# A float32 recommendation tower on one core: who subtracts the rest of layer 0's squares, and behind which instruction

## The chip, the cores and the metric

One core of a Trainium2 chip runs the program. The metric is the device time of one execution in microseconds (us), as the median of several runs. The core has a tensor engine (TensorE, PE in the rows; its weight loads are PEld), a vector engine (VectorE, DVE), a scalar engine (ScalarE, ACT), GpSimd (POOL) and SyncE (SP), which issues most of the DMAs. They run side by side, each through a list of its own, and meet only at semaphores.

## The reference

For 2048 samples, 39 embedding rows of 16 numbers are gathered from 39 tables: `e[b, f, d]`. Then follow three layers of a compressed interaction network:

```
x0 = xk = e
for W, b in ((w0, b0), (w1, b1), (w2, b2)):
    z = relu(einsum('bhd,bkd,hks->bsd', x0, xk, W) + b)      # s = 128
    xk, direct = z[:, :64], z[:, 64:]                        # the last layer: direct = z
```

The direct parts are summed over d (256 values per sample), joined with 16 dense numbers, and go through a small perceptron (512, 256, 1). All of it is float32.

## The kernel before

**Tiles and chunks.** A tile is 128 samples (`TB`); of its 16 embedding positions d, four at a time form a chunk of N = 512 columns (4 x 128). There are 16 tiles of 4 chunks, 64 chunks in all. The quarter c = 0 to 3 says which chunk of its tile it is. `Fori` loops run over the tiles in the middle; the first and the last are written out.

**Layers 1 and 2** of a chunk are 20 steps: a step multiplies two rows of x0 (spread over the partitions by DMA, `xb`) with xk on VectorE (`product`, L752, 128 x 1024), and TensorE contracts the product with W. `KIND = "GVPVGPVGVPVGVGVGVGVP"` gives each step's kind. In a P step the float32 product goes to TensorE as it is (L887). In a V or G step it is split: ScalarE rounds it to float32r (`round_`, L558, the high half `Ph`), the remainder (`Pl`, the low half) is subtracted by VectorE in a V step (L757) and by GpSimd in a G step (`low`, L414), and TensorE takes the high half with two weights (L897) and the low half with one (L907). VectorE's order is the step's product first and then the low half of the step before, where that is a V step. So the low half of step 18 comes behind the product of step 19 and ahead of the next chunk's first product. Steps 6 to 9 already belong to layer 1 of the next chunk. At step 8 ScalarE evacuates layer 1's result: `direct1` (L570), which waits for TensorE's steps up to 5, then `upper` (L561) and `lower` (L564), which VectorE needs for step 10. The code has ScalarE do this ahead of the rounding of step 8.

**Layer 0** is computed from squares: (a + b) squared holds the product of a and b. For the chunk two ahead, TensorE transposes the embedding into the bank `aux_ps` at step 0 (L863), ScalarE copies it out (L540, L541), TensorE makes sums of pairs in the same bank (`sums`, L870, at `SUM_AT`), ScalarE squares them (`square`, L545, at `SQUARE_AT`), and TensorE contracts the squares with w0 (`contract0`, L875, L877, at `CONTRACT_AT`). There are 780 pairs, which is six groups of 128 (float32) and a rest of 12. The rest goes in float32r: the sums of the 12 pairs stand three times in the bank, at partitions 0, 32 and 64, `sqx` is the rounded square of 76 partitions (L549), and its rows 0 to 11 are then replaced by the remainder of the rounding: the exact square, minus the rounded one. One matmul (L877), at step 19, takes it all.

**What sets the order around the change.** All of it is written out by hand in step numbers. `rest_squares` (ScalarE, step 18, ahead of the rounding of step 18) squares the bank into `sqx` and, once more, its first 12 rows into SBUF (`rest_sq`, L550). `rest_low` (L420) is GpSimd's subtraction, `sqx[LOWS] = rest_sq - sqx[LOWS]`, at `REST_AT = 17` behind the low half of step 17 and ahead of the gathers of steps 18 and 19 and of the low half of step 0. For the first two chunks, in the prologue, VectorE does it (L764). TensorE's `contract0` of the rest waits for `rest_ready`; the next transposes wait for `rest_square`, since they overwrite the bank. In quarter 1 the next tile's embedding is split too: ScalarE's L531 at step 15 and L534 at step 17, GpSimd's L424 at step 18.

Of the kernel before, what the change touches and what calls it, by code (L numbers as in the profile page):

```python
# [13 lines left out]
GAP = 32  # L14
# [14 lines left out]
LOWS = slice(0, REST)  # L29
ROWS = slice(2 * GAP, 2 * GAP + NF)  # L30
assert 0 < REST <= GAP
# [16 lines left out]
CONTRACT_AT = [6, 8, 10, 12, 14, 16, 19]  # L48
REST_AT = 17
DIRECT0_AT, UPPER0_AT, LOWER0_AT, RELU2_AT, DIRECT1_AT, RELU1_AT = 2, 3, 4, 5, 8, 8  # L50
# [82 lines left out]
def build(nc, ids, tables, x0_dram, sel0_d, inc_d, w0a_d, w0b_d, w1_d, w2_d, b_d, dense_d, wt1_d, wx_d, bt1_d, wt2_d, bt2_d,  # L133
          wt3_d, out):
    ctx = ExitStack()
    with ctx:
# [16 lines left out]
        sel0 = sb("sel0", [128, 2 * N], F32R)  # L153
        rows = sb("rows", [ROWS.stop, N])
        sq = sb("sq", [R0, 2, N])
# [18 lines left out]
        bt2 = sb("bt2", [128, H2 // 128])  # L174

        rows_sb, rest_sq = rows[ROWS, :], rows[LOWS, :]

# [144 lines left out]
        def _(sp):  # L322
# [9 lines left out]
            def write_rows(T, c):  # L332

                sp.wait_ge(rows_ready, T * CPT + c + 1)
                sp.dma_start(x0_dram[c % SCRATCH, 0:NF, :], rows_sb).then_inc(rows_written, 16)
                sp.wait_ge(rows_written, 16 * (T * CPT + c + 1))
                sp.sem_inc(rows_settled, 1)
# [54 lines left out]
        def _(pool):  # L392
# [23 lines left out]

            def rest_low(T, chunk):
                pool.wait_ge(rest_high, T * CPT + chunk + 1)
                pool.wait_ge(rest_square, T * CPT + chunk + 1)
                pool.tensor_tensor(sqx[LOWS, :], rest_sq, sqx[LOWS, :], ALU.subtract).then_inc(rest_ready, 1)  # L420

            def low_emb(T):
# [48 lines left out]
            def tile(T, ref, fields, first=False, last=False):  # L471

                todo = [list(f) for f in fields]
                for c in range(CPT):
                    for k in range(STEPS):
                        if KIND[k] == "G" and (CPT * ref + c, k) in STEPSET:
                            low(T, ref, c, k)
                        if k == REST_AT and not (last and c >= 2):
                            rest_low(T, c + 2)
                        if (c, k) == NEXT_IDS_AT and todo[2]:  # L480
                            next_ids(T + 2)
                        part = min(c, 1) if (c, k) < NEXT_IDS_AT else 2
                        n = GATHERS[c].count(k) + (first and c == 0 and k in FOLD1_AT)
                        for f in todo[part][:n]:
                            gather(f)
                        todo[part] = todo[part][n:]
                        if c == 0 and not first and k in FOLD1_AT:
                            if k == FOLD1_AT[0]:
                                pool.wait_ge(z2_read, T * CPT)
                            fold1(T - 1, FOLD1_AT.index(k) + 1)  # L490
                        if c == 2 and k == FOLD1A_AT:
                            pool.wait_ge(z2_read, T * CPT + 2)
                            fold1(T, 0)
                        if c == 1 and k == FOLD0A_AT:
                            pool.wait_ge(z0_read, T * CPT + 2)
                            pool.wait_ge(z1_read, T * CPT + 2)
                            fold0(T, 0)
                        if c == CPT - 1 and k in FOLD0_AT:
                            if k == FOLD0_AT[0]:
                                pool.wait_ge(z0_read, T * CPT + CPT)  # L500
                                pool.wait_ge(z1_read, T * CPT + CPT)
                            fold0(T, FOLD0_AT.index(k) + 1)
                        if c == 1 and k == LOW_AT and not last:
                            low_emb(T + 1)
# [16 lines left out]
        def _(act):  # L521
# [15 lines left out]
            def copy_x(T, number):  # L537

                act.wait_ge(aux_ready, T * PER["aux"] + number + 1)
                act.activation(rows_sb, aux_ps[0:NF], ACT.Copy).then_inc(rows_ready, 1)  # L540
                act.activation(x2[:, :], aux_ps[0:R2], ACT.Copy).then_inc(aux_read, 1)  # L541
# [5 lines left out]
            def rest_squares(T, chunk, number, bank=aux_ps):  # L547
                act.wait_ge(aux_ready, T * PER["aux"] + number + 1)
                act.activation(sqx[:, :], bank[0:REST0], ACT.Square).then_inc(rest_high, 1)  # L549
                act.activation(rest_sq, bank[LOWS], ACT.Square).then_inc(rest_square, 1)  # L550

# [163 lines left out]
        def _(dve):  # L715
# [44 lines left out]

            def rest_low(chunk):
                dve.wait_ge(rest_high, chunk + 1)
                dve.wait_ge(rest_square, chunk + 1)
                dve.tensor_tensor(sqx[LOWS, :], rest_sq, sqx[LOWS, :], ALU.subtract).then_inc(rest_ready, 1)  # L764

# [11 lines left out]

            rest_low(0)
            dve.wait_ge(xk1_ready, 1)
            waiting = None  # L780
            for s in range(PRE):
                dve.wait_ge(xb_in[s], 32)
                product(0, 0, -1, L1B + s)
                if s == PRE - 1:
                    rest_low(1)
                if waiting:
# [5 lines left out]
            def tile(T, ref, first=False, last=False):  # L792
                for c in range(CPT):
                    end = last and c == CPT - 1
                    waiting = None
                    for k in range(STEPS):
# [15 lines left out]
                        if waiting:  # L812
                            low(*waiting)
                        waiting = (T, ref, c, k) if KIND[k] == "V" else None
                    if waiting:
                        low(*waiting)
# [43 lines left out]
        def _(pe):  # L860
# [100 lines left out]
            def tile(T, ref, first=False, last=False):  # L961
                late = None
                for c in range(CPT):
                    no0 = last and c >= 2
                    for k in range(STEPS):
                        number = AUX * (c + 2)
                        aux = T * PER["reads"] + READS * (c + 2)
                        if k == TRANSPOSE_AT and not no0:
                            pe.wait_ge(emb_full, T + 1 + (c + 2) // CPT)
                            pe.wait_ge(emb_low, T + 1 + (c + 2) // CPT)  # L970
                            pe.wait_ge(aux_read, aux)
                            pe.wait_ge(rest_square, T * CPT + c + 2)
                            transposes((c + 2) % CPT)
# [125 lines left out]
```

## Time and profile before

| | |
|---|---|
| median of 3 runs | 2473.49 us (2471.82 to 2473.76) |
| the profiled execution | 2473.12 us, its span 2471.3 us |
| busy: TensorE, its weight loads | 2417.4 us (98%), 1646.7 us (67%) |
| busy: VectorE | 2224.4 us (90%) |
| busy: ScalarE | 1733.9 us (70%) |
| busy: GpSimd | 1948.2 us (79%) |
| mean granted clock of TensorE | 0.993 of full |

The span is the time from the first to the last instruction of the profiled execution; the profiled execution's own time is 1.8 us longer. Busy is the time in which an engine has an instruction of the program under way. Matmuls are pipelined and their ends are modelled, so a matmul's row is longer than its share of TensorE; the weight loads' starts show TensorE's pace better. "Idle before" in a row is time in which the engine stood still ahead of the instruction, with what ended it.

### The profile page before, as it was taken

The numbers are of one execution on the slowest core, as the hardware profiler recorded it, in microseconds if no ns is written. First come the engines' busy times: TensorE is split into PE (matmuls) and PEld (weight loads), VectorE is DVE, ScalarE is ACT, GpSimd is POOL, SyncE is SP. The second block draws the span as 40 slices with busy tenths as digits, with TensorE's granted clock in tenths as the row PEclk, the third lists the DMA queues.
The fourth block names the chain that finished last, engine by engine and source line by source line (L and its number), as shares of the span: only waits on it lengthen the run. The fifth ranks groups of instructions, "written<-read, shape, count | busy, mean of one in ns | idle before, by whom it ended". The sixth has DMA issues, their size and how long they took to land.

```text
span 2471.3 us, 33379 instructions
## 1 busy us (share of the span) xinstructions
PE 2417.4 (98%) x8886; PEld 1646.7 (67%) x8886; DVE 2224.4 (90%) x1894; ACT 1733.9 (70%) x2203; POOL 1948.2 (79%) x1331
## 2 busy tenths in 40 slices
PE   5899999999999999999999999999999999999989
PEld 2566666666666666666666666666666666666656
DVE  1599999999989999999999999899999999999993
ACT  1677777777767777767777776677777777777655
POOL 6688888888878888888888888788888888866550
PEclk9899999999999999999999999999999999999999
DMA  3778667766856866776786677586677667667730
GB/s 75 156 146 175 140 137 163 154 140 143 174 121 143 172 136 139 165 154 137 147 169 138 139 166 152 115 171 146 137 154 165 138 136 173 146 136 153 164 92 1
DMA packets 214717, 352.61 MB, mean 143 GB/s; under 512 B 34382, under 2 KB 47566, under 8 KB 214588
## 3 DMA queue, kind: packets, MB, share of 16 engines
q1 hardware_dynamic: 194717, 347.07, 65.2%
q0 software_dynamic: 19968, 5.15, 2.4%
q8 instruction: 16, 0.26, 0.0%
q14 instruction: 16, 0.13, 0.0%
HBM read 346.97 MB, written 5.12 MB: 142 GB/s over the span
## 4 chain that ended last, share of the span: by engine, by line
PE 57%; POOL 25%; issue 13%; DVE 3%; ACT 1%; POOLq 0%; DMA 0%; ACTq 0%; DVEq 0%
PE ps L897 21%; PE ps L907 11%; POOL Pl L414 11%; PE ps L887 10%; POOL emb L408 10%; PE ps L875 8%; PE ps L870 3%; POOL dir L443 2%; DVE ps L752 1%; DVE P L752 1%; DVE Pl L757 1%; POOL sqx L420 1%; PE ps L1014 1%; PE ps L863 1%; PE ps L1024 1%
## 5 line engine op out<-in xcount | busy, mean ns | idle before, releaser
L414 POOL TENSOR_TENSOR Pl<-P,Ph 128x1024 fp32r<-128x1024 f32 x448 | 1074.6, 2399 | 285.9 <-ACT Ph L558 260.7
L897 PE MATMUL ps<-Ph,wh 128*128 128x512 f32 x2048 | 965.1, 471 | 9.7 <-ACT Ph L558 9.7
L558 ACT ACTIVATE Ph<-ps 128x1024 fp32r<-128x1024 f32 x576 | 590.3, 1025 | 405.9 <-DVE ps L752 394.3
L752 DVE TENSOR_TENSOR P<-xb,ps 128x1024 f32<-128x1024 f32 x704 | 854.5, 1214 | 3.2 <-DMA xb<-x_dram 3.2
L757 DVE TENSOR_TENSOR Pl<-ps,Ph 128x1024 fp32r<-128x1024 f32 x576 | 705.4, 1225 | 113.5 <-ACT Ph L558 94.7
L897 PE MATMUL ps<-Ph,wl 128*128 128x512 f32 x1920 | 755.3, 393 | 0.0
L907 PE MATMUL ps<-Pl,wh 128*128 128x512 f32 x2048 | 741.9, 443 | 8.2 <-POOL Pl L414 8.2
L408 POOL DMA_INDIRECT emb<-tbl_in,idx x624 | 600.4, 962 | 171.4 <-issue 146.0
L752 DVE TENSOR_TENSOR ps<-xb,ps 128x1024 f32<-128x1024 f32 x576 | 706.9, 1227 | 30.3 <-issue 10.2
L558 ACT ACTIVATE Ph<-P 128x1024 fp32r<-128x1024 f32 x448 | 473.9, 1058 | 186.5 <-DVE P L752 120.5
L907 PEld LDWEIGHTS ps<-Pl,wh 128*128 128x128 f32 x2048 | 384.2, 188 | 200.9 <-issue 118.1
L897 PEld LDWEIGHTS ps<-Ph,wh 128*128 128x128 f32 x2048 | 387.3, 189 | 179.8 <-issue 90.7
L887 PE MATMUL ps<-P,wp 128*128 128x512 f32 x1024 | 481.3, 591 | 0.0
L897 PEld LDWEIGHTS ps<-Ph,wl 128*128 128x128 f32 x1920 | 363.7, 189 | 154.7 <-issue 89.6
L875 PE MATMUL ps<-sq,w 128*128 128x512 f32 x768 | 396.9, 599 | 0.3 <-ACT sq L545 0.3
L887 PEld LDWEIGHTS ps<-P,wp 128*128 128x128 f32 x1024 | 193.5, 189 | 144.4 <-issue 123.6
L545 ACT ACTIVATE sq<-ps 128x512 f32<-128x512 f32 x384 | 223.9, 583 | 17.3 <-PE ps L870 11.0
L870 PE MATMUL ps<-x,sel 78*128 78x512 f32 (+1 forms) x448 | 183.9, 412 | 5.0 <-issue 3.7
L875 PEld LDWEIGHTS ps<-sq,w 128*128 128x128 f32 x768 | 145.2, 190 | 36.5 <-ACT sq L545 3.5
L443 POOL TENSOR_TENSOR dir<-dir 128x512 f32<-128x512 f32 (+1 forms) x128 | 148.4, 1159 | 5.6 <-ACT dir L573 4.9
L870 PEld LDWEIGHTS ps<-x,sel 78*128 78x128 f32 (+1 forms) x448 | 82.7, 185 | 27.5 <-issue 7.0
L561 ACT ACTIVATE ps<-ps,bias 64x512 f32<-64x512 f32 x128 | 83.5, 652 | 4.2
(84 smaller groups left out, 893.7 us busy)
## 6 DMA issues: line engine op xcount, KB each, us to landing
xb<-x_dram SPq DMA_DIRECT2D x1280, 256.0 KB
emb<-tbl_in,idx POOLq DMA_INDIRECT x624
x_dram<-rows SPq DMA_DIRECT2D x64, 78.0 KB
xb<-w_in SPq DMA_DIRECT2D x16, 128.0 KB
xb<-wt_in SPq DMA_DIRECT2D x2, 512.0 KB, 4.3
xb<-dense_in SPq DMA_DIRECT2D x1, 768.0 KB, 5.3
wp<-w_in SPq DMA_DIRECT2D x4, 128.0 KB
xb<-w0a_in SPq DMA_DIRECT2D x1, 448.0 KB
```

The costliest lines, as they stand in the source:

```text
L408: pool.indirect_dma_start(emb[:, f, :], None, tables[f], bass.IndirectOffsetOnAxis(ap=idx[:, f:f + 1], axis=0))\
L414: pool.tensor_tensor(Pl[:, h_slot(ref, c, k)], P[:, p_slot(ref, c, k)], Ph[:, h_slot(ref, c, k)], ALU.subtract).then_inc(low_pool, 1)
L443: pool.tensor_tensor(o_, x, y, ALU.add).then_inc(done, 1)
L545: act.activation(sq[:, t % 2, :], bank, ACT.Square).then_inc(aux_read, 1)
L558: act.activation(Ph[:, h_slot(ref, c, k)], p, ACT.Copy).then_inc(rounded, 1)
L752: dve.tensor_tensor(p, xb[:, x], xk.unsqueeze(1).broadcast_to([128, 2, N]), ALU.mult)\
L757: dve.tensor_tensor(Pl[:, h_slot(ref, c, k)], p_ps, Ph[:, h_slot(ref, c, k)], ALU.subtract)\
L870: pe.matmul(bank[0:r], sel[:, t, 0:r], x2[:, :], start=True, stop=True)\
L875: m = pe.matmul(z0_ps[:, bank], w0[:, t, :], sq[:, t % 2, :], start=start, stop=stop)
L887: m = pe.matmul(z_of(c, k), wp[:, PLAIN.index(k), j, :], P[:, p_slot(ref, c, k), j, :], start=k in (L1B, L2) and j == 0, stop=stop and j == 1)
L897: pe.matmul(z_of(c, k), w[:, q, j, :], Ph[:, h_slot(ref, c, k), j, :], start=k in (L1B, L2) and i + j == 0, stop=False)
L907: m = pe.matmul(z_of(c, k), wh[:, q, j, :], Pl[:, h_slot(ref, c, k), j, :], start=False, stop=stop and j == 1)
```

## The change

GpSimd no longer does the subtraction; VectorE does it in every chunk, at step 19, behind the product of step 19 and the low half of step 18, so directly ahead of the next chunk's first product. Its exact square comes from PSUM: ScalarE's second square writes the bank's first 12 rows in place and no longer an SBUF buffer, and waits for its first square, which reads the same rows. TensorE's transposes wait for the subtraction, since it now reads the bank. The SBUF buffer `rows` shrinks to the 39 rows that the copy of x needs.

```diff
-ROWS = slice(2 * GAP, 2 * GAP + NF)
-REST_AT = 17
+REST_AT = 19
...
-        rows = sb("rows", [ROWS.stop, N])
+        rows_sb = sb("rows_sb", [NF, N])
-        rows_sb, rest_sq = rows[ROWS, :], rows[LOWS, :]
... GpSimd
-            def rest_low(T, chunk):
-                pool.wait_ge(rest_high, T * CPT + chunk + 1)
-                pool.wait_ge(rest_square, T * CPT + chunk + 1)
-                pool.tensor_tensor(sqx[LOWS, :], rest_sq, sqx[LOWS, :], ALU.subtract).then_inc(rest_ready, 1)
-                        if k == REST_AT and not (last and c >= 2):
-                            rest_low(T, c + 2)
... ScalarE, rest_squares
                 act.activation(sqx[:, :], bank[0:REST0], ACT.Square).then_inc(rest_high, 1)
-                act.activation(rest_sq, bank[LOWS], ACT.Square).then_inc(rest_square, 1)
+                act.wait_ge(rest_high, T * CPT + chunk + 1)
+                act.activation(bank[LOWS], bank[LOWS], ACT.Square).then_inc(rest_square, 1)
... VectorE
-            def rest_low(chunk):
-                dve.wait_ge(rest_high, chunk + 1)
-                dve.wait_ge(rest_square, chunk + 1)
-                dve.tensor_tensor(sqx[LOWS, :], rest_sq, sqx[LOWS, :], ALU.subtract).then_inc(rest_ready, 1)
+            def rest_low(T, chunk, bank=aux_ps):
+                dve.wait_ge(rest_square, T * CPT + chunk + 1)
+                dve.tensor_tensor(sqx[LOWS, :], bank[LOWS], sqx[LOWS, :], ALU.subtract).then_inc(rest_ready, 1)
-            rest_low(0)
+            rest_low(0, 0, early_ps[0][0])
-                    rest_low(1)
+                    rest_low(0, 1, early_ps[1][0])
                         if waiting:
                             low(*waiting)
                         waiting = (T, ref, c, k) if KIND[k] == "V" else None
+                        if k == REST_AT and not (last and c >= 2):
+                            rest_low(T, c + 2)
... TensorE, ahead of the transposes
-                            pe.wait_ge(rest_square, T * CPT + c + 2)
+                            pe.wait_ge(rest_ready, T * CPT + c + 2)
```

## Rows read from the trace of the kernel before

**Rows 1.** The page: span, busy times, the chain that ended last.
```profile
span 2471.3 us, 33379 instructions
PE 2417.4 (98%) x8886; PEld 1646.7 (67%) x8886; DVE 2224.4 (90%) x1894; ACT 1733.9 (70%) x2203; POOL 1948.2 (79%) x1331
PE ps L897 21%; PE ps L907 11%; POOL Pl L414 11%; PE ps L887 10%; POOL emb L408 10%; PE ps L875 8%; PE ps L870 3%; POOL dir L443 2%; DVE ps L752 1%; DVE P L752 1%; DVE Pl L757 1%; POOL sqx L420 1%; PE ps L1014 1%; PE ps L863 1%; PE ps L1024 1%
```

**Rows 2.** Busy time by stretch, four chunks: stretch and length, busy PE, PEld, DVE, ACT, POOL.
```profile
1255.06:1291.06 36.00, 36.00 (x136) 24.80 (x135) 34.26 (x30) 26.04 (x33) 30.80 (x23) 1.00 0.71 148
1291.06:1327.19 36.13, 36.13 (x136) 24.79 (x134) 33.99 (x30) 27.51 (x35) 28.06 (x20) 1.00 0.74 152
1327.19:1363.30 36.11, 36.11 (x136) 24.65 (x135) 34.48 (x30) 26.03 (x33) 32.12 (x22) 1.00 0.71 146
1363.30:1399.29 35.99, 35.99 (x136) 24.80 (x134) 34.25 (x30) 26.04 (x33) 30.69 (x22) 1.00 0.73 155
sum 144.23, PE 144.23 PEld 99.04 DVE 136.98 ACT 105.62 POOL 121.67; mean PE 36.06 PEld 24.76 DVE 34.24 ACT 26.41 POOL 30.42
```

**Rows 3.** Groups by line and form: count, busy us, mean ns, idle before.
```profile
L420 POOL TENSOR_TENSOR sqx<-rows,sqx 12x512 fp32r<-12x512 f32 x62 | 79.6, 1284 | 0.0
...
L764 DVE TENSOR_TENSOR sqx<-rows,sqx 12x512 fp32r<-12x512 f32 x2 | 1.4, 676 | 5.3 <-ACT rows L550 5.3
```

**Rows 4.** Timeline of VectorE from 1249.5 us: start, duration, instruction, idle before.
```profile
1252.91 1.23 DVE L757 TENSOR_TENSOR Pl<-ps,Ph 128x1024 fp32r<-128x1024 f32 x1
1254.05 1.21 DVE L752 TENSOR_TENSOR P<-xb,ps 128x1024 f32<-128x1024 f32 x1
...
1263.49 1.22 DVE L752 TENSOR_TENSOR ps<-xb,ps 128x1024 f32<-128x1024 f32 x1
...
1270.67 1.23 DVE L757 TENSOR_TENSOR Pl<-ps,Ph 128x1024 fp32r<-128x1024 f32 x1 [1.18 <-ACT Ph L558]
```

**Rows 5.** Timeline of ScalarE over the same chunk: roundings of steps 18, 4, 6, 7; direct1.
```profile
1251.84 1.03 ACT L558 ACTIVATE Ph<-ps 128x1024 fp32r<-128x1024 f32 x1 [0.53 <-DVE ps L752]
...
1261.80 1.05 ACT L558 ACTIVATE Ph<-P 128x1024 fp32r<-128x1024 f32 x1
1262.75 0.67 ACT L573 ACTIVATE dir<-ps,bias 128x512 f32<-128x512 f32 x1
...
1264.83 1.02 ACT L558 ACTIVATE Ph<-ps 128x1024 fp32r<-128x1024 f32 x1 [0.93 <-DVE ps L752]
...
1266.22 1.06 ACT L558 ACTIVATE Ph<-P 128x1024 fp32r<-128x1024 f32 x1
1267.54 0.68 ACT L570 ACTIVATE dir<-ps,bias 64x512 f32<-64x512 f32 x1 [0.26 <-PE ps L907]
```

**Rows 6.** Timeline of the weight loads: the rest's contraction, and step 4's high half.
```profile
1255.06 0.19 PEld L877 LDWEIGHTS ps<-sqx,w0x 76*128 76x128 f32 x1
...
1263.33 0.19 PEld L897 LDWEIGHTS ps<-Ph,wh 128*128 128x128 f32 x1
```

**Rows 7.** Timeline of ScalarE at direct1 of the three chunks that follow.
```profile
1303.58 0.68 ACT L570 ACTIVATE dir<-ps,bias 64x512 f32<-64x512 f32 x1 [0.30 <-issue]
...
1338.60 1.06 ACT L558 ACTIVATE Ph<-P 128x1024 fp32r<-128x1024 f32 x1
1339.80 0.68 ACT L570 ACTIVATE dir<-ps,bias 64x512 f32<-64x512 f32 x1
...
1375.78 0.68 ACT L570 ACTIVATE dir<-ps,bias 64x512 f32<-64x512 f32 x1 [0.26 <-PE ps L907]
```

**Rows 8.** Timeline of ScalarE at a quarter 1's end: second square, rounding of step 18.
```profile
1179.56 0.57 ACT L550 ACTIVATE rows<-ps 12x512 f32<-12x512 f32 x1
1180.04 1.00 ACT L558 ACTIVATE Ph<-ps 128x1024 fp32r<-128x1024 f32 x1
```

**Rows 9.** Timeline of VectorE at the same place: the low half of step 18.
```profile
1181.07 1.23 DVE L757 TENSOR_TENSOR Pl<-ps,Ph 128x1024 fp32r<-128x1024 f32 x1 [0.40 <-ACT Ph L558]
```

**Rows 10.** Timeline of the weight loads in the quarter 2 that follows: step 0's low half.
```profile
1187.69 0.30 PEld L907 LDWEIGHTS ps<-Pl,wh 128*128 128x128 f32 x2 [0.39 <-POOL Pl L414]
```

More of the change, by code:

```diff
@@ L334, in write_rows @@
                 sp.wait_ge(rows_ready, T * CPT + c + 1)
-                sp.dma_start(x0_dram[c % SCRATCH, 0:NF, :], rows_sb).then_inc(rows_written, 16)
+                sp.dma_start(x0_dram[c % SCRATCH, 0:NF, :], rows_sb[:, :]).then_inc(rows_written, 16)
                 sp.wait_ge(rows_written, 16 * (T * CPT + c + 1))
@@ L539, in copy_x @@
                 act.wait_ge(aux_ready, T * PER["aux"] + number + 1)
-                act.activation(rows_sb, aux_ps[0:NF], ACT.Copy).then_inc(rows_ready, 1)
+                act.activation(rows_sb[:, :], aux_ps[0:NF], ACT.Copy).then_inc(rows_ready, 1)
                 act.activation(x2[:, :], aux_ps[0:R2], ACT.Copy).then_inc(aux_read, 1)
```

## The prediction

> **What bounds the kernel now.** I read the page first. TensorE is busy for 98% of the span, VectorE for 90%, GpSimd for 79%, ScalarE for 70%; the chain of work that ended last is 57% TensorE and 25% GpSimd, with GpSimd's sqx subtraction (the instruction that is moved) at 1% [rows 1]. Two readings offer themselves: TensorE is full and nothing else matters, or GpSimd is on the path and its relief is a gain. The busy time by stretch decides for the first: cut at the weight load of L877, which occurs once per chunk, four chunks in a row take 36.00, 36.13, 36.11 and 35.99 us (sum 144.23), and in each TensorE's busy time equals the stretch [rows 2]. So 62 of the 64 chunks run at TensorE's own pace of 35.99 us, with about 0.27 us lost per four chunks. The third thing to ask is how far the others are behind that pace, and VectorE's 90% does not say it: its idle time may lie in a place that a longer VectorE cannot use. So the last views are the timelines of VectorE, ScalarE and the weight loads over one chunk.
>
> VectorE's timeline: around the chunk's end it runs without a break. The low half of step 18 starts at 1252.91 and the next chunk's first product at 1254.05, 0.09 us before the former ends [rows 4]. Its only real stop in the first half of the chunk is 1.18 us before the low half of step 8, at 1270.67, for ScalarE [rows 4]. ScalarE's timeline shows what that stop consists of: the rounding of step 6 (1264.83) starts when VectorE's product of step 6 (1263.49) is done; then a square and the rounding of step 7 follow back to back (1266.22 to 1267.28), and then direct1 (L570) starts at 1267.54, after 0.26 us for TensorE [rows 4, 5]. After direct1 come upper, lower and the rounding of step 8, for which VectorE waits. So VectorE's 1.18 us are not free: from the first product of a chunk to the next chunk's first product there runs one unbroken chain through VectorE and ScalarE, with its only link to TensorE at direct1, and **the slack of that chain is the wait at direct1**, not VectorE's idle time. Where ScalarE does not wait for anybody, it starts 0.10 us before its former instruction ends (L573 at 1262.75 behind a rounding that ends at 1262.85) [rows 5], so the slack is 0.26 + 0.10 = 0.36 us. In the three following chunks it is 0.30, 0.14 and 0.26 (1339.80 against an end at 1338.60 + 1.06 = 1339.66 for the middle one) plus 0.10 each [rows 7]. Sum over four chunks: 0.96 + 0.40 = **1.36 us**.
>
> **The change part by part.**
>
> GpSimd loses one subtraction per chunk, 62 of 1284 ns, 79.6 us of busy time [rows 3]. What it could free is the wait for a GpSimd low half: in the quarter after the embedding's low part, TensorE's load of the low half of step 0 idles 0.39 us for it (1187.69) [rows 10]. With one instruction of 1.28 us fewer in front, this goes. It is most of the 0.27 us per four chunks above TensorE's pace, so the gain is at most 0.27 x 15.5 = 4.2 us, and only as long as TensorE stays the bound. Elsewhere GpSimd's earlier finish gives nothing; its next low half waits for the rounding of step 0 anyway, which becomes later.
>
> VectorE gets one subtraction per chunk, 12 x 512 with one input in PSUM. The nearest row is its own form of it in the prologue, 12 x 512 from SBUF, 676 ns (L764) [rows 3]; the nearest with PSUM is the low half of twice the columns, 1.23 us, of which half is 0.61 [rows 4]. Fixed cost does not halve, so I take 0.68; the ends are 0.61 and 0.69. It waits for a square that ScalarE ended over 2 us before, so I let it start as products do, 0.09 us early: **0.60 us added to VectorE per chunk** (ends: 0.52, and 0.73 if it starts 0.04 behind the one before it, as low halves that follow a product do). Nothing covers it: behind it in VectorE's order are the next chunk's products, and through them the whole chain above.
>
> The Trainium skill says in "VectorE: DVE Perf Modes", section The DRAIN you can't avoid, that the next operation does not start until the pipe is empty, and further on that an instruction which is not held may start earlier. The rows at hand go with the second (0.09 us of overlap); by the first the sum below would be that of rival B.
>
> ScalarE: its second square of the rest now writes the PSUM rows that the first one reads, and waits for it. From 0.10 us of overlap to a start some 0.03 us behind the former end (round after a wait) is 0.12 us more; ends 0 and 0.25. In three quarters of four the rounding of step 18 has 0.53 us of idle time before it [rows 5], which hides this. In the quarter with the next tile's embedding it has none: 1179.56 and 1180.04 overlap, and VectorE waits 0.40 us for that rounding [rows 8, 9]. There the 0.12 goes onto the chain: 0.12 per four chunks. Its destination (PSUM for SBUF) I cost at nothing; both have the same 512 columns.
>
> TensorE: the rest's contraction (L877) now waits for VectorE. VectorE's low half of step 18 ends at 1254.14, so the new one ends at about 1254.73, before the load at 1255.06 [rows 4, 6]: hidden by 0.3 us. In the embedding's quarter it ends near 1182.29 + 0.12 + 0.60 = 1183.0, about when L877 comes; if TensorE is late there, it is by less than the chain's own delay, so nothing is added. The transposes' new wait for rest_ready is behind L877, which has waited for the same value: nothing. With the chain 0.60 late, the tightest of TensorE's loads is the high half of step 4: at 1263.33, its rounding ends at 1262.85, 0.48 apart [rows 5, 6]. So TensorE waits for the first time at step 4, and then keeps the chain's pace. No DMA and no SyncE entry is moved; the loads of xb hang on products that all come at the same later pace. The buffers' new layout costs nothing.
>
> **Sum** for four chunks: 4 x 0.60 + 0.12 - 1.36 = 1.16 us over today's 144.23. That is 36.35 us per chunk against 36.06. Times 15.5 (62 chunks): 18.0 us. The profiled execution took 2473.12 (its span 2471.3); the median of the runs is 2473.49, 0.4 above it. Forecast for the median: 2473.49 + 18.0 = **2491.5 us**, 0.7% slower. With VectorE's term at 0.52: 4 x 0.52 + 0.12 - 1.36 = 0.84, 13 us, 2486.5; ScalarE's ends move it by 2 us.
>
> **The rivals.**
>
> B, the subtraction does not overlap: it costs 0.73 per chunk, the sum is 4 x 0.73 + 0.12 - 1.36 = 1.68, times 15.5 = 26 us: 2499.5. For it: it reads what another engine wrote behind a semaphore. Against it: the semaphore is long set.
>
> C, TensorE stays the bound: the chain has more slack than I read (a wait ahead of direct1 that gives way, so that 0.60 is absorbed), and GpSimd's relief counts. Its place is direct1; it decides if the slack there is over 0.60 instead of 0.36. Then four chunks take 4 x 35.99 = 143.96, and the time is 2473.49 - 4.2 = 2469.3. For it: TensorE's busy time fills every chunk, VectorE has 1.2 us idle per chunk. Against it: that idle time ends with ScalarE's back-to-back run.
>
> D, the other side outright: GpSimd is on the path as far as the chain of work says, 1% of 2471 us, and what leaves it is gained: 25 us, 2449. For it: 25% of the chain is GpSimd's. Against it: TensorE shows no idle time behind L420 in three of four chunks, so the chain's share is a choice between equals. The Trainium skill says in "GPSIMD Engine Reference", in its opening and in section 3.1 (Elementwise), that VectorE does such arithmetic about twice as fast and is to be preferred. The rows agree on the operation, 1284 against 676 ns [rows 3]; what they do not show is that the saved time lies on the path.
>
> **How the numbers follow.** A has 0.65, B 0.15, C 0.15, D 0.03; 0.02 is left for a slower end that I do not name, such as more stretches at the lower of TensorE's two clocks now that it waits a little in each chunk. A measurement of this kernel tells about 0.2% (5 us) from no change. C at -0.17% lies just within it, so I give 0.13 of its 0.15 to "same" and 0.02 to "faster"; D makes that 0.05. A and B and the rest are slower: 0.82. The range runs from a half-absorbed A, 2480, to B with its bound, 2501; C and D, 0.18, stay outside. A's own range is 2486 to 2495.
>
> **What would show it.** Right: the stretches between two L877 loads at some 36.3 us; VectorE's new instruction at 0.67 to 0.69 us, starting 0.09 before the low half of step 18 ends; no wait, or nearly none, at direct1; new waits of TensorE's high half (L897) for ScalarE, around step 4, in nearly every chunk; GpSimd with over 70 us less busy time and more waiting for roundings. Wrong: chunks of 35.99 with direct1 still waiting for TensorE (C); a start gap of the new instruction above zero (B); L877 waiting for VectorE in each chunk, which would mean that I misread where VectorE stands at the chunk's end.

## The result, and the profile after

The change is slower, as forecast: 2493.19 us as the median of 4 runs (2492.53 to 2494.95) against 2473.62 beside them, ratio 1.0083 with a 95% interval of 1.0069 to 1.0096. Medians and ratios here and below leave out two executions at a much lower granted clock, one of 2592.63 us (clock 0.901) of the kernel with the swapped instructions and one of 6188.15 us (0.37) of the kernel before. The profiled execution went from a span of 2471.3 to 2493.1 us. The new file is shorter, so its lines have other numbers: L743 stands for L752 (product), L748 for L757 (VectorE's low half), L549 for L558 (rounding), L561 for L570 (direct1), L411 for L414, L869 for L877 (the rest's contraction), L889 and L899 for L897 and L907. The subtraction is L754.

The page's head and its chain of work that ended last, answering to [rows 1]:

```profile
span 2493.1 us, 33304 instructions
PE 2439.4 (98%) x8886; PEld 1639.4 (66%) x8886; DVE 2260.8 (91%) x1956; ACT 1728.7 (69%) x2203; POOL 1875.2 (75%) x1269
DVE 44%; ACT 21%; issue 20%; PE 11%; POOL 3%; ACTq 1%; DVEq 1%; DMA 0%; POOLq 0%
DVE ps L743 17%; DVE Pl L748 17%; ACT Ph L549 15%; DVE P L743 10%; PE ps L889 3%; POOL emb L405 2%; PE ps L867 2%; PE ps L899 2%; ACT dir L561 2%; ACT ps L552 2%; PE ps L879 1%; ACT ps L555 1%; PE ps L1006 1%; POOL Pl L411 1%; ACTq L547 1%
```

TensorE's busy share says nothing: it is 98% as before. The chain does: before it was TensorE for 57% and GpSimd for 25%, now it is VectorE for 44%, ScalarE for 21% and TensorE for 11%. GpSimd's busy time fell by 73.0 us. The busy time by stretch over four chunks, cut at the weight load of L869, answers to [rows 2]:

```profile
1265.10:1301.44 36.34, 36.34 (x136) 24.63 (x134) 34.83 (x31) 25.93 (x33) 29.44 (x21) 1.00 0.72 149
1301.44:1338.28 36.84, 36.72 (x137) 24.64 (x135) 34.83 (x31) 27.45 (x35) 27.60 (x18) 1.00 0.73 151
1338.28:1374.62 36.34, 36.31 (x134) 24.57 (x134) 34.82 (x31) 25.94 (x33) 30.26 (x22) 1.00 0.69 143
1374.62:1410.97 36.35, 36.35 (x136) 24.64 (x134) 34.83 (x31) 25.94 (x33) 29.63 (x22) 1.00 0.72 153
sum 145.87, PE 145.72 PEld 98.48 DVE 139.30 ACT 105.26 POOL 116.93; mean PE 36.43 PEld 24.62 DVE 34.83 ACT 26.32 POOL 29.23
```

Four chunks take 145.87 us instead of 144.23, 1.64 more, with 136 matmuls each as before. "PE busy" still fills them nearly, 145.72 of 145.87, although the matmuls are the same and the chunks longer. So it can't show that TensorE no longer sets the pace; the chain above and the waits below do.

The timeline of VectorE at a chunk's end, with the new instruction between the low half of step 18 and the next product:

```profile
1263.23 1.22 DVE L748 TENSOR_TENSOR Pl<-ps,Ph 128x1024 fp32r<-128x1024 f32 x1
1264.38 0.67 DVE L754 TENSOR_TENSOR sqx<-ps,sqx 12x512 fp32r<-12x512 f32 x1
1264.97 1.20 DVE L743 TENSOR_TENSOR P<-xb,ps 128x1024 f32<-128x1024 f32 x1
```

The product starts 1.74 us after the low half instead of 1.14 [rows 4]: 0.60 us added, with overlaps of 0.07 and 0.08 us, near the 0.09 that was assumed. The timeline of ScalarE at direct1 of the same chunk, answering to [rows 5]:

```profile
1277.14 1.06 ACT L549 ACTIVATE Ph<-P 128x1024 fp32r<-128x1024 f32 x1
1278.22 0.68 ACT L561 ACTIVATE dir<-ps,bias 64x512 f32<-64x512 f32 x1
```

No wait for TensorE is left in front of L561; but it starts at 1278.22, 0.02 us **behind** the rounding's end (1277.14 + 1.06 = 1278.20), not 0.10 us ahead of it. The same gap of 0.02 to 0.03 us stands there in 60 of 63 chunks. TensorE's side, from the timeline of the weight loads in that chunk and from the waits of the whole execution:

```profile
1269.88 0.30 PEld L899 LDWEIGHTS ps<-Pl,wh 128*128 128x128 f32 x2 [0.36 <-POOL Pl L411]
...
1273.81 0.19 PEld L889 LDWEIGHTS ps<-Ph,wh 128*128 128x128 f32 x1 [0.30 <-ACT Ph L549]
```

```profile
PEld ps L889 <- ACT Ph L549: 64.8, 228, 1.5
PEld ps L899 <- POOL Pl L411: 34.6, 74, 3.9
...
PEld ps L869 <- DVE sqx L754: 7.0, 15, 0.6
```

TensorE now waits at step 0 for GpSimd's low half and at step 4 for the rounding. The low half of step 0 is waited for in 55 chunks, 0.38 us in the mean, and the rounding of step 4 in 55, 0.30 us. Most of the others of the 228 waits at L889 lie later in the chunk and are 0.24 us long, which is also the gap before loads that wait for nothing. These waits are the symptom: by the chain above, both engines are late because VectorE is. The wait for the rest itself (L869) comes 15 times, once per tile but one.

### The profile page after: what moved, and what is told of

It is laid out like the page before. It is cut to its first block, busy times and chain, and to the rows that moved or that the text cites. A ratio compares the mean times of both kernels' runs of the same rounds, so it can differ in the third digit from the quotient of the medians.

```text
span 2493.1 us, 33304 instructions
## 1 busy us (share of the span) xinstructions
PE 2439.4 (98%) x8886; PEld 1639.4 (66%) x8886; DVE 2260.8 (91%) x1956; ACT 1728.7 (69%) x2203; POOL 1875.2 (75%) x1269
## 4 chain that ended last, share of the span: by engine, by line
DVE 44%; ACT 21%; issue 20%; PE 11%; POOL 3%; ACTq 1%; DVEq 1%; DMA 0%; POOLq 0%
DVE ps L743 17%; DVE Pl L748 17%; ACT Ph L549 15%; DVE P L743 10%; PE ps L889 3%; POOL emb L405 2%; PE ps L867 2%; PE ps L899 2%; ACT dir L561 2%; ACT ps L552 2%; PE ps L879 1%; ACT ps L555 1%; PE ps L1006 1%; POOL Pl L411 1%; ACTq L547 1%
## 5 line engine op out<-in xcount | busy, mean ns | idle before, releaser
L411 POOL TENSOR_TENSOR Pl<-P,Ph 128x1024 fp32r<-128x1024 f32 x448 | 1077.0, 2404 | 383.5 <-ACT Ph L549 374.7
L889 PE MATMUL ps<-Ph,wh 128*128 128x512 f32 x2048 | 971.4, 474 | 9.2 <-ACT Ph L549 9.1
L549 ACT ACTIVATE Ph<-ps 128x1024 fp32r<-128x1024 f32 x576 | 591.1, 1026 | 417.4 <-DVE ps L743 409.9
L743 DVE TENSOR_TENSOR P<-xb,ps 128x1024 f32<-128x1024 f32 x704 | 853.0, 1212 | 2.6 <-DMA xb<-x_dram 2.6
L748 DVE TENSOR_TENSOR Pl<-ps,Ph 128x1024 fp32r<-128x1024 f32 x576 | 705.5, 1225 | 100.3 <-ACT Ph L549 82.2
L889 PE MATMUL ps<-Ph,wl 128*128 128x512 f32 x1920 | 756.6, 394 | 0.0
L899 PE MATMUL ps<-Pl,wh 128*128 128x512 f32 x2048 | 748.0, 446 | 7.8 <-POOL Pl L411 7.3
L743 DVE TENSOR_TENSOR ps<-xb,ps 128x1024 f32<-128x1024 f32 x576 | 706.2, 1226 | 29.7 <-ACT ps L555 11.9
L549 ACT ACTIVATE Ph<-P 128x1024 fp32r<-128x1024 f32 x448 | 473.9, 1058 | 222.1 <-DVE P L743 203.3
L899 PEld LDWEIGHTS ps<-Pl,wh 128*128 128x128 f32 x2048 | 381.4, 189 | 212.7 <-issue 118.6
L889 PEld LDWEIGHTS ps<-Ph,wh 128*128 128x128 f32 x2048 | 387.3, 189 | 193.7 <-ACT Ph L549 64.8
L889 PEld LDWEIGHTS ps<-Ph,wl 128*128 128x128 f32 x1920 | 363.9, 190 | 152.5 <-issue 89.3
```

Source lines behind the costliest of these rows:

```text
L411: pool.tensor_tensor(Pl[:, h_slot(ref, c, k)], P[:, p_slot(ref, c, k)], Ph[:, h_slot(ref, c, k)], ALU.subtract).then_inc(low_pool, 1)
L549: act.activation(Ph[:, h_slot(ref, c, k)], p, ACT.Copy).then_inc(rounded, 1)
L743: dve.tensor_tensor(p, xb[:, x], xk.unsqueeze(1).broadcast_to([128, 2, N]), ALU.mult)\
L748: dve.tensor_tensor(Pl[:, h_slot(ref, c, k)], p_ps, Ph[:, h_slot(ref, c, k)], ALU.subtract)\
L889: pe.matmul(z_of(c, k), w[:, q, j, :], Ph[:, h_slot(ref, c, k), j, :], start=k in (L1B, L2) and i + j == 0, stop=False)
L899: m = pe.matmul(z_of(c, k), wh[:, q, j, :], Pl[:, h_slot(ref, c, k), j, :], start=False, stop=stop and j == 1)
```

## The experiments

All runs are compared with the kernel before on the same chip; its medians there were 2471.1 to 2473.2 us.

**Is it VectorE's time at all?** Nobody subtracts.

```diff
-                        if k == REST_AT and not (last and c >= 2):
-                            rest_low(T, c + 2)
...
-                                pe.wait_ge(rest_ready, T * CPT + c + 3)
+                                pe.wait_ge(rest_square, T * CPT + c + 3)
```

> Nobody subtracts: the remainder of the rest's rounding is left out, sqx keeps the rounded square in its first 12 rows, and TensorE waits for the second square alone. It is the kernel before with GpSimd 79.6 us of busy time lighter and VectorE no heavier. Theory (the chain through VectorE and ScalarE is what the change overloaded, and GpSimd's relief is worth only TensorE's wait for the low half in quarter 2): four chunks at 4 x 35.99 = 143.96, 2469.5 us. Rival (GpSimd's relief is worth nothing at all, the 0.39 us gap before that weight load is caught up): 2473.6. Rival (GpSimd is on the path by its share of the chain of work): 2450.

2468.29 us (11 runs), ratio 0.9981 (0.9972 to 0.9990). The same four chunks by stretch:

```profile
sum 144.05, PE 144.05 PEld 99.28 DVE 136.96 ACT 105.61 POOL 116.82; mean PE 36.01 PEld 24.82 DVE 34.24 ACT 26.40 POOL 29.20
```

0.18 us per four chunks under before, which makes 2.8 us over 15.5 such groups, and 4.9 us in all. In the two profiles most of the rest lies in two chunks in which GpSimd stands still ahead of a gather: 41.12 and 40.87 us here, 42.01 and 42.52 before. Those chunks differ from trace to trace (39.3 to 43.2 us over all kernels), and that leaving out the subtraction shortens them is not shown. So GpSimd's relief gives some 3 us, 5 at the most. The rival that went by GpSimd's share of the chain of work is out.

**Is it ScalarE's part?** The kernel before, with the second square waiting for the first.

```diff
                 act.activation(sqx[:, :], bank[0:REST0], ACT.Square).then_inc(rest_high, 1)
+                act.wait_ge(rest_high, T * CPT + chunk + 1)
                 act.activation(rest_sq, bank[LOWS], ACT.Square).then_inc(rest_square, 1)
```

> The kernel before, with ScalarE's second square waiting for its first (GpSimd still subtracts, from SBUF). Theory: the 0.12 us fall into 0.53 us of idle time in three quarters and into a slack of about 0.11 in the fourth: 2473.6, at most 2475.5. Rival (ScalarE's longer pair of squares, ahead of the rounding of step 18, is what costs): most of the 20 us, 2485 to 2493.

2473.09 us, ratio 1.0001 (0.9992 to 1.0010): nothing. ScalarE's wait costs nothing by itself.

**Is it the handshake with TensorE?** The same work with the two VectorE instructions swapped.

```diff
                         product(T, ref, c, k)
+                        if k == REST_AT and not (last and c >= 2):
+                            rest_low(T, c + 2)
                         if waiting:
                             low(*waiting)
                         waiting = (T, ref, c, k) if KIND[k] == "V" else None
-                        if k == REST_AT and not (last and c >= 2):
-                            rest_low(T, c + 2)
```

> The change, with VectorE's subtraction ahead of the low half of step 18 instead of behind it. Theory (the chain): behind the product of step 19 VectorE has 0.05 us for ScalarE anyway, so 0.45 instead of 0.60 is added in three quarters, and in quarter 1, where it waits 0.4 us and more for the rounding of step 18, nothing but ScalarE's 0.12. Against 0.84 us of slack per four chunks that is 0.62 us, some 7 to 10 us: 2480 to 2483. Rival (TensorE's wait for the rest is the cost; now the value is there over 1 us earlier): 2470 to 2474. Rival (VectorE's busy time counts as such): 2493.

2479.70 us, ratio 1.0033 (1.0020 to 1.0046), as the chain has it. The rest's value is there earlier and TensorE waits for it nowhere, yet more than a third of the loss stays. What went is the part that VectorE now does while it would wait for ScalarE anyway; its busy time is nearly that of the change, 138.98 us against 139.30. By stretch:

```profile
sum 144.91, PE 144.91 PEld 98.59 DVE 138.98 ACT 105.27 POOL 116.86; mean PE 36.23 PEld 24.65 DVE 34.75 ACT 26.32 POOL 29.21
```

**How large is the slack?** The change, with the subtraction over fewer columns: `sqx[LOWS, 0:W]`, `bank[LOWS, 0:W]`, W = 128 and 256.

```diff
-                dve.tensor_tensor(sqx[LOWS, :], bank[LOWS], sqx[LOWS, :], ALU.subtract).then_inc(rest_ready, 1)
+                dve.tensor_tensor(sqx[LOWS, 0:W], bank[LOWS, 0:W], sqx[LOWS, 0:W], ALU.subtract).then_inc(rest_ready, 1)
```

> The change, with VectorE subtracting only 128 of the 512 columns (the remainder of the others is left out). The instruction should take about 0.27 us, 0.18 beyond the overlap. Theory: the wait of 0.26 us before direct1 has a floor of 0.03, so 0.23 us per chunk are free; 0.18 fits in it in three quarters, and quarter 2 has 0.11: 2470 to 2474. Rival (each us of VectorE costs, in proportion to its added time): 2473.6 + 19.6 x 0.18 / 0.60 = 2479.5. Rival (the cost is TensorE's wait for the rest): 2470, as the value comes 0.4 us earlier, but then the order of the two on VectorE should matter too, which another run asks.

> The change, with VectorE subtracting 256 of the 512 columns (the others' remainder is left out). About 0.40 us, 0.31 beyond the overlap. Theory: 4 x 0.31 + 0.12 - 0.84 = 0.52 us per four chunks, 5 to 8 us: 2479 to 2481. Rival in proportion: 2473.6 + 19.6 x 0.31 / 0.60 = 2484.

2472.50 us, ratio 0.9999 (0.9990 to 1.0008), and 2477.40, ratio 1.0023 (1.0014 to 1.0032). The instruction by itself (view of one tile, min/median/max ns), and then the sum of the busy times by stretch over four chunks; W = 128 comes first, then W = 256:

```profile
L754 DVE TENSOR_TENSOR sqx<-ps,sqx x64: 268/269/278, 67.9 to 2341.6; 12x128 fp32r<-12x128 f32 x64
```

```profile
sum 144.29, PE 144.29 PEld 99.03 DVE 137.67 ACT 105.28 POOL 116.84; mean PE 36.07 PEld 24.76 DVE 34.42 ACT 26.32 POOL 29.21
```

```profile
L754 DVE TENSOR_TENSOR sqx<-ps,sqx x64: 400/402/412, 68.1 to 2345.6; 12x256 fp32r<-12x256 f32 x64
```

```profile
sum 144.83, PE 144.80 PEld 98.78 DVE 138.24 ACT 105.22 POOL 116.87; mean PE 36.20 PEld 24.69 DVE 34.56 ACT 26.30 POOL 29.22
```

With 0.09 us of overlap taken off, VectorE gets 0, 0.18, 0.31 and 0.58 us per chunk in the four kernels (nobody, 128, 256, 512 columns; the last three also have ScalarE's 0.12 us in quarter 1), and four chunks take 144.05, 144.29, 144.83 and 145.87. The steps are 0.24 for 4 x 0.18 = 0.72 us of VectorE, then 0.54 for 0.52, then 1.04 for 1.08. Most of the first 0.18 us per chunk is free and from there on each us is paid in full. That is a slack with a kink. Over the kernel before (144.23), the chain's sum with a slack of 0.84 us per four chunks, 4 x the added time + 0.12 - 0.84, gives 144.23, 144.75 and 145.91 for 128, 256 and 512 columns, where 144.29, 144.83 and 145.87 were measured. A charge in proportion to VectorE's time would make them 0.56, 0.41 and 0.85.

**What is the slack's floor?** The change, with direct1 on all 128 partitions, from partition 0.

```diff
-                act.activation(dir0[hi, c, :], z1_ps[hi, c % 2], ACT.Relu, bias=bias[hi, 1:2]).then_inc(z1_read, 1)
+                act.activation(dirx[:, :], z1_ps[:, c % 2], ACT.Relu, bias=bias[:, 1:2]).then_inc(z1_read, 1)
```

> The change, with direct1 reading and writing all 128 partitions (from partition 0) into a buffer of its own instead of 64 partitions from partition 64; layer 1's direct features are left at zero. In the trace of the change direct1 starts 0.03 us behind the rounding ahead of it in nearly every chunk, where other instructions start 0.10 ahead. Theory (ScalarE does not overlap where the start partition changes): the gap becomes -0.10, 0.13 us per chunk leave the chain, 8 us: 2485. Rival (it waits for TensorE or for its semaphores): the gap stays and so does 2493.

2480.72 us, ratio 1.0036 (1.0023 to 1.0049): about 12 us less than the change, more than expected. Layer 1's direct features are left at zero here. ScalarE's timeline from the rounding of step 7 to that of step 8, and the sum of four chunks:

```profile
1270.32 1.06 ACT L550 ACTIVATE Ph<-P 128x1024 fp32r<-128x1024 f32 x1
1271.27 0.69 ACT L562 ACTIVATE dirx<-ps,bias 128x512 f32<-128x512 f32 x1
1271.99 0.65 ACT L553 ACTIVATE ps<-ps,bias 64x512 f32<-64x512 f32 x1
1272.67 0.65 ACT L556 ACTIVATE ps<-ps,bias 64x512 f32<-64x512 f32 x1
1273.26 1.01 ACT L550 ACTIVATE Ph<-ps 128x1024 fp32r<-128x1024 f32 x1
```

```profile
sum 144.94, PE 144.91 PEld 98.65 DVE 139.29 ACT 104.49 POOL 116.78; mean PE 36.23 PEld 24.66 DVE 34.82 ACT 26.12 POOL 29.20
```

direct1 now starts 0.11 us ahead of the rounding's end, and the rounding of step 8 starts 0.06 ahead of the end of L556, in the change 0.03 behind it. Two overlaps came for one edit. By the medians over the chunks the two gaps went from 0.025 behind to 0.112 and 0.063 ahead: 0.137 + 0.088 = 0.225 us per chunk, 0.90 per four, measured 145.87 - 144.94 = 0.93.

The edit changes the start partition and the number of partitions, 64 to 128. The change itself holds a test that separates them: ScalarE's copy of the 39 rows of x wrote from partition 64 before and writes from partition 0 now, and is otherwise the same. The copy and the one behind it, before and in the change:

```profile
1258.96 0.59 ACT L540 ACTIVATE rows<-ps 39x512 f32<-39x512 f32 x1
1259.57 0.59 ACT L541 ACTIVATE x<-ps 78x512 fp32r<-78x512 f32 x1
```

```profile
1269.78 0.58 ACT L530 ACTIVATE rows_sb<-ps 39x512 f32<-39x512 f32 x1
1270.26 0.58 ACT L531 ACTIVATE x<-ps 78x512 fp32r<-78x512 f32 x1
```

The second copy, which waits for nothing, started 0.02 us behind the first one's end and now starts 0.10 us ahead of it, in all 64 chunks of each trace. So it is where the operands start, not how many partitions they have.

**What does the PSUM operand do?** The subtraction on VectorE at the same place, from SBUF, ScalarE as before:

```diff
+                        if k == REST_AT and not (last and c >= 2):
+                            rest_low(T, c + 2)
...
                 dve.tensor_tensor(sqx[LOWS, :], rest_sq, sqx[LOWS, :], ALU.subtract).then_inc(rest_ready, 1)
```

> The kernel before, with only the subtraction moved to VectorE at the same place as in the change, reading the exact square from SBUF; ScalarE as before. Theory: VectorE's 0.60 us per chunk is the whole cost, 2491, some 2 us under the change for ScalarE's 0.12 in quarter 1. Rival (ScalarE's part costs): 2475 or less. Should VectorE with two SBUF inputs be held up by GpSimd's subtractions, which the change's PSUM operand would avoid, its instruction is longer than 0.67 us in some chunks and the time above 2493.

2519.53 us, ratio 1.0188 (1.0174 to 1.0202), far above the main expectation, and by the path that the last sentence left open. VectorE's and GpSimd's timelines at a quarter 1's end:

```profile
1203.94 2.37 DVE L762 TENSOR_TENSOR sqx<-rows,sqx 12x512 fp32r<-12x512 f32 x1
1206.24 1.20 DVE L750 TENSOR_TENSOR P<-xb,ps 128x1024 f32<-128x1024 f32 x1
```

```profile
1203.36 2.40 POOL L424 TENSOR_TENSOR emb<-emb,emb_h 128x624 f32<-128x624 f32 x1
```

VectorE's instruction began 0.58 us into GpSimd's low part of the embedding and ended 0.55 us after it (1206.31 against 1205.76): it stood still for the rest of it. It took 2.35 to 2.48 us in 15 chunks, once per tile but one, and 0.85 to 0.97 us in 13 more, beside one of GpSimd's sums over d (mostly 0.47 us long); in the others it took 0.67 us. From PSUM the same instruction took 668 to 679 ns in all 64 chunks, though in 15 of them it ran wholly inside GpSimd's low part of the embedding, as at 1337.56 us inside 1336.82 to 1339.24. The Trainium skill, "SBUF — State Buffer", section Who interferes with whom, says that a VectorE instruction with two SBUF inputs contends with a GpSimd instruction that reads SBUF; by that rule, the trace agrees. A second run moves the partner away, with `HIGH_AT, LOW_AT` = 13, 15 instead of 15, 18.

> VectorE's subtraction with both inputs in SBUF, as in the run that took 2519.5 us, but with the embedding's split moved as above, so that GpSimd's low part of the embedding no longer runs beside quarter 1's end. There each of those instructions took 2.4 us instead of 0.67. Theory (VectorE is held up by the GpSimd instruction that runs beside it): quarter 1's instruction falls to 0.67 to 0.96 us, 1.4 to 1.7 us per tile, 2493 to 2499. Rival (something else of quarter 1 makes it long, the embedding's DMA or ScalarE): it stays at 2.4 and the time at 2519.

2496.57 us, ratio 1.0097 (1.0081 to 1.0112), and the instruction:

```profile
L762 DVE TENSOR_TENSOR sqx<-rows,sqx x64: 668/670/1171, 68.0 to 2367.0; 12x512 fp32r<-12x512 f32 x64
```

With the embedding's part moved away no chunk is left at 2.4 us; 15 are still at 0.95 to 1.17 us, each beside another GpSimd instruction. It is the partner on GpSimd. So of the change's two halves, PSUM as the source is right and the engine is wrong.

**Is there a version that beats both?** First, the rest ahead of the six full groups, so that its double square and its subtraction fall into idle time in the chunk's middle (GpSimd, step 8).

```diff
-                            t = SQUARE_AT.index(k)
-                            if t < FULL0:
-                                square(T, aux + 1 + t, t)
+                            n = SQUARE_AT.index(k)
+                            if n:
+                                square(T, aux + 1 + n, n - 1)
...
+                        if k == REST_CONTRACT_AT and not no0:
+                            pe.wait_ge(rest_ready, T * CPT + c + 3)
+                            contract0(FULL0, c % 2, False, False)
```

> The kernel before with the rest's sums, squares first in the chunk (steps 3 and 6) instead of last, GpSimd's subtraction at step 8 and the rest's contraction at step 13; nothing is left out. Theory: the double square falls into 0.9 us of ScalarE's idle time ahead of the rounding of step 6 and GpSimd's 1.28 us into its idle time, quarter 1's end is lighter on ScalarE and GpSimd, TensorE alone bounds: four chunks at 143.96, 2469.5. Rival (GpSimd is too late for the low half of step 11, or the sum of step 5 waits for the second square): 2475 or more.

2471.85 us, ratio 1.0003 (0.9994 to 1.0011). No gain. The stretches' sum is 144.15; the waits show why it isn't 143.96:

```profile
PEld ps L898 <- ACT Ph L559: 52.7, 88, 1.4
```

With one contraction fewer ahead of step 8, TensorE comes there sooner and waits for that step's rounding.

Second, the kernel before with the embedding's split moved off quarter 1's end, `HIGH_AT, FULL_AT, LOW_AT` = 13, 17, 15, then 12, 17, 12.

> The kernel before with the next tile's embedding split earlier in quarter 1: ScalarE's rounding of it at step 13 instead of 15, GpSimd's low part at step 15 instead of 18; GpSimd still subtracts the rest. Nothing is left out. Theory: what GpSimd could give was only TensorE's wait in quarter 2 for the low half of step 0, and that comes from the low part of the embedding in front of it; moved off, four chunks take 144.0 instead of 144.2, 2469 to 2471. Rival (the gathers have not landed by step 13, ScalarE waits, and all behind it): above 2475.

2478.29 us, ratio 1.0022 (1.0013 to 1.0031): slower, by two causes. At step 15 GpSimd's 2.4 us push the low half of step 17 and the subtraction back, and TensorE waits for the rest in quarter 1:

```profile
1332.61 0.19 PEld L877 LDWEIGHTS ps<-sqx,w0x 76*128 76x128 f32 x1 [0.61 <-POOL sqx L420]
```

That costs 0.24 us per tile, some 3.6 us: quarters 1 and 2 take 36.60 and 35.87 us instead of 36.12 and 36.11. The rival's cause, late gathers, came too, once for 3.22 us and once for 0.32 us, and the chunk of the first took 39.84 us where the kernel before has 36.59:

```profile
301.20 0.72 ACT L531 ACTIVATE emb_h<-emb 128x624 fp32r<-128x624 f32 x1 [3.22 <-DMA emb<-tbl_in,idx]
```

> The kernel before with the next tile's embedding split at step 12 of quarter 1: ScalarE's rounding into its 0.9 us of idle time ahead of the rounding of step 12, GpSimd's low part behind the low half of step 11, where GpSimd otherwise waits 1.6 us. At step 15 (the run of 2478.3 us) it had pushed the low half of step 17 and the rest's subtraction 0.5 us back, and TensorE waited 0.61 us for the rest. Theory: here nothing of quarter 1's end is pushed, TensorE waits for neither, four chunks take 144.05 as in the run that leaves the subtraction out, and the time is 4 us under the kernel before, 2468 to 2470. Rival (the gathers have not landed by then): above 2475.

2475.74 us, ratio 1.0019 (1.0010 to 1.0028). Half of the theory held: four chunks took 144.07. But in two of the tiles ScalarE stood waiting for gathers, 5.23 us in one of them (the four chunks by stretch, then ScalarE's timeline):

```profile
sum 144.07, PE 144.07 PEld 99.14 DVE 136.93 ACT 105.74 POOL 121.69; mean PE 36.02 PEld 24.78 DVE 34.23 ACT 26.44 POOL 30.42
```

```profile
299.85 0.72 ACT L531 ACTIVATE emb_h<-emb 128x624 fp32r<-128x624 f32 x1 [5.23 <-DMA emb<-tbl_in,idx]
```

In these two tiles, here as in the run before, GpSimd had stood still ahead of a gather 11 to 18 us earlier (3.14 us at 288.2 and 6.34 us at 721.0 here). Whether such late gathers make up the whole of the nearly 5 us by which the median is slower is open; only one execution was profiled, and its span was 2471.5. No version tried beats the kernel before.

## Why the prediction was right, and where not

**What bounds the kernel** was right: TensorE at the pace of a full list, and behind it a chain through VectorE and ScalarE whose slack is read at direct1. The kink of the narrow subtractions shows that slack; so do the swap, and the chain of work that ended last, which went from TensorE and GpSimd to VectorE and ScalarE.

**VectorE's term**, 0.60 us per chunk from 0.68 less 0.09, was right: 0.67 long, 0.60 added. B's premise, no overlap, was wrong.

**ScalarE's 0.12 in quarter 1** was right as a term. ScalarE's and VectorE's timelines of the change at a quarter 1's end, answering to [rows 8, 9]:

```profile
1334.27 0.58 ACT L539 ACTIVATE sqx<-ps 76x512 fp32r<-76x512 f32 x1
1334.89 0.55 ACT L541 ACTIVATE ps<-ps 12x512 f32<-12x512 f32 x1
```

```profile
1336.41 1.23 DVE L748 TENSOR_TENSOR Pl<-ps,Ph 128x1024 fp32r<-128x1024 f32 x1 [0.54 <-ACT Ph L549]
```

The second square starts 0.04 us behind the first one's end, and VectorE waits 0.54 instead of 0.40 us for the rounding of step 18. By itself it costs nothing (2473.09); it counts only once the chain is the bound.

**The buffers' new layout** was put at nothing, and that came out right, though not because nothing changed: the copy of x that starts at partition 0 now and the one behind it save ScalarE some 0.2 us per chunk (the two gaps were 0.02 us behind each and are 0.07 and 0.10 ahead). The rounding behind them waits for VectorE's product, before and now, and takes up all of it.

**The slack was mis-sized, and this is the step that failed**: "so the slack is 0.26 + 0.10 = 0.36 us", summed to 1.36 us over four chunks. The 0.10 was borrowed from L573, which reads and writes all 128 partitions from partition 0. direct1 reads and writes from partition 64, and starts 0.02 to 0.03 us behind its predecessor however long its operands have been there. The slack is 0.96 - 4 x 0.03 = 0.84, and the sum 4 x 0.60 + 0.12 - 0.84 = 1.68, where 1.64 was measured and 1.16 forecast. It happens to be rival B's figure, 1.68, by another cause.

**The total was nearer than its terms deserved,** and that is luck. 1.64 x 15.5 would be 25 us; from the third of the 64 loads of L869 to the last, the change took 2232.0 us and the kernel before (L877) 2212.3, so 19.7. The rest was given back in chunks where GpSimd, not the chain, held TensorE up. Before, one of these took 42.02 us; its stretch, GpSimd's gather in it and TensorE's wait for the low half behind that gather:

```profile
708.42:750.44 42.02, 37.94 (x136) 25.57 (x135) 35.31 (x31) 28.74 (x36) 29.29 (x20) 0.96 0.67 138
```

```profile
718.64 0.96 POOL L408 DMA_INDIRECT emb<-tbl_in,idx  x1 [6.38 <-issue]
```

```profile
724.53 0.30 PEld L907 LDWEIGHTS ps<-Pl,wh 128*128 128x128 f32 x2 [4.90 <-POOL Pl L414]
```

The stretch that answers to it in the change took 39.83 us:

```profile
714.84:754.67 39.83, 36.82 (x136) 24.56 (x134) 34.83 (x31) 27.45 (x35) 27.55 (x18) 1.00 0.66 135
```

and the first chunks of both kernels, which are not in step yet, differ by less than the later ones. The prediction counted 15.5 tiles alike. With its own slack it came to 18.0; with the right slack and the same count it would have said 26, still inside the range.

**TensorE's waits** came as forecast at step 4 (L889 for ScalarE, in 55 chunks) and, which was not forecast, at step 0 for GpSimd's low half. L869's wait in quarter 1 was forecast as about nil and is up to 0.6 us, on an engine that is waiting for the chain anyway.

**The rivals.** C fell with direct1's vanished wait and the narrow subtractions, D with the run in which nobody subtracts.

**GpSimd's relief**, at most 4.2 us with TensorE as the bound, was read too high where it can be followed: 0.27 us per four chunks forecast, 0.18 measured with nobody subtracting, since quarters 1 and 2 take 36.03 us and not 35.99 even then. That the whole execution gave 4.9 us is owed in part to the two chunks with GpSimd's standstills. In the change itself nothing of it is left.

## What to carry to other kernels

When an engine sits at 90% and another at 98%, the question is not whether the 10% would hold the new instruction but where its idle time lies: follow the chain behind it to the one wait that can shrink, and compare that wait with what is added. Here 0.21 us per chunk were free and 0.60 were asked, so moving an instruction to an engine that does it twice as fast lost 0.8%. And measure how far a wait can shrink on the very instruction that waits, not on a neighbour of another shape.

## What the runs showed of the hardware that was not expected

ScalarE starts an instruction that waits for nothing 0.05 to 0.12 us ahead of its predecessor's end where both work from partition 0, and 0.02 to 0.03 us behind it where the start partition changes. (One that waits for what its predecessor has just made starts 0.03 us behind it too, as the second square does.) Moving direct1 from partition 64 to partition 0 took the gap from 0.02 behind to 0.11 ahead, and that of the rounding after L556 from 0.03 behind to 0.06 ahead, though that rounding was not touched: the last instruction before it that wrote SBUF was direct1. The copy of the 39 rows of x, moved from partition 64 to partition 0, did the same to the copy behind it, 0.02 behind to 0.10 ahead. The Trainium skill, "VectorE: DVE Perf Modes", section Two Vector instructions with no wait between them, describes such a hold, by the start quadrant of the last read and write in each memory, for VectorE; these three gaps on ScalarE follow it, which is a reading from two edits and not a test of the whole rule.

VectorE with both inputs in SBUF stood still behind a GpSimd subtraction, 2.37 us for 0.67; with one of them in PSUM it never did, not even in the 15 chunks in which it ran inside that GpSimd instruction (0.67 us).

GpSimd stands still ahead of a gather four times in each execution, for nothing that the profile names: in all 13 traces near 290, 720, 1560 and 1970 us, for 3.0 to 4.1 us at the first and last and 4.5 to 6.4 us at the two between (6.38 us before 718.64 in the kernel before). TensorE waited 4.90 us behind that one, and the granted clock of that chunk was 0.96. Its cause was not looked into.
